# A quantised attention loop: VectorE's copy of turned codes behind a step's second maximum, and a bias addition moved from that loop to the feed-forward

## The reference, cut to what matters

```python
q = quant_act(q, q_alpha, q_zp, 4) * SCALE
k = quant_act(k, k_alpha, k_zp, 4)
v = quant_act(v, v_alpha, v_zp, 4)
attn = jnp.einsum('bhnd,bhmd->bhnm', q, k)
attn = jax.nn.softmax(attn, axis=-1)
attn = quant_act(attn, attn_alpha, attn_zp, 8)   # clip(round(attn / alpha + zp)) to 8 bits
out = jnp.einsum('bhnm,bhmd->bhnd', attn, v)
out = out.transpose(0, 2, 1, 3).reshape(B, N, C)
y = jnp.einsum('bnc,oc->bno', out, wp) + proj_b
...
x = x + y          # x is the program's input
```

## Time and profile before

| what | value |
|---|---|
| median of 3 runs | 777.06 us (776.28 to 779.78) |
| the profiled execution | 775.85 us, span from first to last instruction 774.1 us |
| busy share of the span | PE 81%, DVE 70%, ACT 65%, POOL 31% |
| stage B | from 199.6 us (first scores) to 338.5 us (end of the last codes) |

### The profile page before, as it was taken

How to read it: one execution, slowest core, us unless ns; L and a number is a source line. 1 busy time by engine, 2 the same in 40 slices (tenths; PEclk the granted TensorE clock), 3 DMA queues, 4 the chain that set the end, 5 groups by cost and what they waited for, 6 DMA issues and landing times.

```text
span 774.1 us, 13306 instructions
## 1 busy us (share of the span) xinstructions
PE 626.8 (81%) x4818; PEld 378.4 (49%) x4818; DVE 544.9 (70%) x1123; ACT 501.2 (65%) x1189; POOL 236.1 (31%) x237
## 2 busy tenths in 40 slices
PE   7579987686688988985898978778688889677986
PEld 3322223264255655662655545454467655355754
DVE  7784326737899988958877777649984556977554
ACT  5459997654577877842567657739468547758752
POOL 5030006003388977983200000000154300035410
PEclk9769997899755555577579999989679899969989
DMA  9400000000000000000000000000000000000000
GB/s 283 158 1 1 1 1 1 0 1 0 1 2 1 1 1 1 1 2 0 1 1 2 1 1 2 2 0 1 0 2 2 2 1 0 1 1 2 3 1 27
DMA packets 9204, 9.88 MB, mean 13 GB/s; under 512 B 2890, under 2 KB 7988, under 8 KB 9012
## 3 DMA queue, kind: packets, MB, share of 16 engines
q1 hardware_dynamic: 9140, 9.04, 3.6%
HBM read 8.51 MB, written 0.52 MB: 12 GB/s over the span
## 4 chain that ended last, share of the span: by engine, by line
PE 44%; DVE 34%; ACT 11%; issue 8%; POOL 1%; DMA 1%; ACTq 0%; DVEq 0%; POOLq 0%
PE ps L1452 5%; PE ps L1712 4%; DVE s_nmB L1095 4%; PE ps L1615 4%; PE ps L1695 3%; ACT arena L578 3%; PE ps L1732 3%; PE ps L1523 2%; PE ps L1806 2%; PE ps L1602 2%; PE ps L1495 2%; PE ps L1917 2%; DVE s_nmD L1366 2%; PE ps L1854 2%; PE ps L1440 2%
## 5 line engine op out<-in xcount | busy, mean ns | idle before, releaser
L422 POOL TENSOR_SCALAR arena<-arena,s_rB,s_zpu 128x512 uint8<-128x512 f32 x128 | 116.0, 944 | 34.7 <-DVE s_rB L1068 33.9
L616 ACT ACTIVATE arena<-ps,s_nmB 128x512 f32<-128x512 f32 x128 | 86.6, 683 | 31.4 <-DVE s_nmB L1095 30.8
L638 ACT ACTIVATE arena<-ps,s_nmx 128x512 f32<-128x512 f32 (+3 forms) x128 | 60.7, 527 | 50.1 <-DVE s_nmx L1193 49.7
L1095 DVE TENSOR_REDUCE s_nmB<-ps 128x2 f32<-128x1024 f32 x64 | 77.3, 1217 | 6.6 <-PE ps L1602 6.2
L456 POOL COPY arena<-arena 64x512 f32<-64x512 f32 x16 | 12.4, 773 | 217.5 <-PE ps L1799 215.6
L1188 DVE TENSOR_REDUCE s_nmx<-ps 128x1 f32<-128x512 f32 (+3 forms) x128 | 56.6, 483 | 21.4 <-PE ps L1698 20.9
L578 ACT ACTIVATE arena<-ps 128x1024 f32<-128x1024 f32 x64 | 60.9, 1026 | 6.9 <-PE ps L1507 6.8
L1458 PE MATMUL ps<-ones 128*128 128x512 f16 x150 | 44.2, 446 | 24.0 <-ACT s_rn L569 3.6
L1615 PE MATMUL ps<-cst,arena 128*128 128x128 f32 x256 | 61.0, 417 | 1.7 <-POOL arena L422 0.8
L1615 PEld LDWEIGHTS ps<-cst,arena 128*128 128x128 f32 x256 | 48.8, 218 | 14.7 <-POOL arena L422 8.2
L1602 PE MATMUL ps<-staged 8*128 8x512 f16 x128 | 45.8, 580 | 12.4 <-ACT arena L616 11.5
(11 more groups left out here) (337 smaller groups left out, 1508.0 us busy)
## 6 DMA issues: line engine op xcount, KB each, us to landing
w_d<-in_wqkv SPq DMA_DIRECT2D x2, 768.0 KB
vec<-in_vec SPq DMA_DIRECT2D x1, 1200.0 KB, 10.5
vec<-in_vec SPq DMA_DIRECT2D x1, 960.0 KB, 8.1
w_h<-in_w SPq DMA_DIRECT2D x2, 341.0 KB
x_tok<-in_x SPq DMA_DIRECT2D x1, 512.0 KB, 3.9
arena<-in_w_f SPq DMA_DIRECT2D x2, 256.0 KB, 7.8
rope<-in_rope SPq DMA_DIRECT2D x1, 512.0 KB, 8.9
w_do<-in_wo SPq DMA_DIRECT2D x2, 256.0 KB
```

The source lines that it names most:

```text
L422: nc.gpsimd.tensor_scalar(u8[:, n % 4, j // 2, :, 2 * (j % 2)], prob[:, n % 2, j * 512:j * 512 + 512], sm("rB", 8)[:, c:c + 1], sm("zpu", ...
L616: nc.scalar.activation(prob[:, n % 2, j * 512:j * 512 + 512], ps[:, j, :], ACT.Exp, bias=sm("nmB", 8)[:, c:c + 1], accum_out=sm("sumB", 8) ...
L638: nc.scalar.activation(probC[:, n % 2, at(qt):at(qt) + w], ps[:, bank, col:col + w], ACT.Exp, bias=nmx[:, TB * b + qt, h:h + 1]).then_inc( ...
L1095: free(V.tensor_reduce(sm("nmB", 8)[:, c:c + 2], ps[:, 2 * half:2 * half + 2, :], X, ALU.max, negate=True), "maxB")
```

## The change

On VectorE, `codes_half(n - 3)` moves out of the loop over the two halves, so that it stands behind the second maximum instead of between the rates and the second maximum. And the two additions x + proj_b leave steps 9 and 10 of stage B and stand in stage M, behind the evacuations of the first feed-forward matrix. No instruction is added or taken away, and the streams of PE, ACT, POOL and SP are the same, instruction by instruction.

```diff
@@ stage M @@
                 taken(t, V.scalar_tensor_tensor(out=hid1[:, t, :], in0=ps[:, t % 6, :], scalar=sm("us")[:, t:t + 1],
                                                 in1=v_("b_f1"), op0=ALU.mult, op1=ALU.add))
+            for b in range(B):
+                xb = x[:, TB * b:TB * b + TB, :]
+                add(xb, xb, per_tile(v_("proj_b"), TB))
             dve.wait_ge(sem["fn"], 1)
@@ stage B, step n @@
                         if half == 0 and n >= 1:
                             rates(n - 1)
-                        if half == 0 and n >= 3:
-                            codes_half(n - 3)
+                    if n >= 3:
+                        codes_half(n - 3)
...
                     if n == H + 6:
                         values_b(0)
-                    if n in (9, 10):
-                        xb = x[:, TB * (n - 9):TB * (n - 8), :]
-                        add(xb, xb, per_tile(v_("proj_b"), TB))
                     if n == 3:
                         scale_b(1)
```

## The result

The changed kernel took 780.16 us in the median of 20 runs (777.28 to 783.42), the kernel before 775.43 in 20 runs on the same chip (773.56 to 779.78). The ratio of the means is 1.0057, with 95% interval [1.0041, 1.0073]: slower by 4.4 us of 775.4 (3.2 to 5.7). The forecast, +3.3 us on 777.06, is a ratio of 1.0043.

The account below looks back on a forecast made before the run. It took TensorE at 1.2 GHz to bound stage B, three other engines nearly as full; +4.0 for the copy and -0.7 for the additions gave +3.3 on 777.06, so 780.4 us, range 774 to 785.5.

Parts of the forecast that it names:

- The maximum loop: Stage B, two-step loop through VectorE, ScalarE and TensorE: with the copy 7.60 us, 8.20 in the group-copy step.
- the count over four steps: Stage B from a group-copy step: four steps take 16.05 instead of 15.47, so the copy's 0.58 is paid once.
- Eight steps times 0.5: Stage B steps 3, 5, 7, 10, 14, 18, 20, 22 pay 0.5 each, +4.0; 6 and 26 nothing.
- The additions: Leaving stage B's steps 9 and 10 gives -0.7 us, bounds 0 and -1.4; in stage M's idle gap they cost nothing.
- Zero for the transposes: Stage B: the moved copy ends before TensorE's second half of transposes needs it, so no cost was taken.
- one of the prediction's own signs of being wrong: In the changed kernel's profile: a wait of TensorE's transposes on VectorE's copy appears.
- The spare of 0.12: Stage B: copy ends at S + 1.89, TensorE needs it at S + 2.01, S being its second scores' end.
- The rival: Stage B: transposes wait for the copy, 0.2 in each of 29 steps, +5.8 more, 786 us; chance 0.13.
- TensorE's waits on exponentials: Stage B: TensorE's stops for ScalarE, 11.5 us before, would grow by about 4.
- The faster rival: Stage B: earlier second maximum brings rates earlier, GpSimd waits less; -3.1, 774.0 us, at most -8.3; chance 0.14.
- GpSimd as the pace: Stage B: GpSimd paces the steps and hides the delay; -0.5, 776.6 us; chance 0.18.
- a floor of 3.79 a step: Stage B: rates cannot overtake codes in flight by the port rule, so GpSimd needs at least 3.79 us a step.

Follow-up runs that it names:

- job steps: Changed kernel, copy behind the second maximum only in steps 3, 5, 6, 7, 10, 14, 18, 20, 22, 26; ratio 1.007, stage B 137.54 us.
- additions only: Changed kernel with the copy of codes back in front of the second maximum; ratio 1.0032 against the kernel before, stage B 133.28 us.
- free steps: Changed kernel, copy behind the second maximum only in the 19 steps without another VectorE job there; ratio 1.0012, stage B 133.70 us.

## Why the prediction was right, point by point

- **The maximum loop** held. Second maximum 0.04 behind its scores (within 0.1 said), next first maximum 0.61 later (0.6), two steps 8.19 (8.20). In the group-copy step, ScalarE's exponentials are what TensorE waits for. What covers the copy in the other steps was named wrongly: not the first maximum's wait, since step 13's first maximum starts 0.72 behind its scores, for 0.18 before. The slack lies behind it, between the exponentials and TensorE's next first scores, as the count over four steps had it (11.10 against 11.70).
- **Eight steps times 0.5** gave the right sum by unequal parts. The delay of the second maximum against before rose by 0.8 at step 3, 0.85 at 5, 0.25 at 7, fell by 0.17 at 10 (0.55 for the copy less the additions' 0.72), rose by 0.69 at 14 and at 18, and by 0 at 20 and 0.1 at 22. That is 3.2, for 3.3 forecast with the additions taken off. One error is in taking a job's own duration as fixed: at steps 3, 5, 7, 20 and 22 it changed with the move (last section). That 6 pays nothing was right, that 26 does was not: it paid 0.54 in "job steps". Its second maximum stood 0.65 behind its scores before only because TensorE ran at 1.00 there; in "additions only", at 0.50, it is 0.10. In the pair of before and after the larger gain of after's own stretch hides this price.
- **The additions** were right: -0.72 for -0.7, and free in stage M.
- **Zero for the transposes** failed in part, and with it one of the prediction's own signs of being wrong came true: TensorE's transposes do wait for VectorE's copy. The spare of 0.12 left out the 0.15 from the copy's end to the fifth transpose, so seven steps waited 0.14 each. Two of these lie in the four steps of the chain above: the first ran ahead of the wait for ScalarE, which took it up (8.19), the second (272.93) is the 0.12 over the forecast's 16.05. The rival had the mechanism; its price, 0.2 in 29 steps or 5.8, is refuted by 7 x 0.14 = 1.0.
- **TensorE's waits on exponentials** grew by 2.2, not by about 4. I had left the additions out of that figure: net, stage B's 3.3 was to be found. Full stops hold 2.2 of it, the seven longer transposes the other 1.0, which the trace counts as busy.
- **The faster rival** fell: GpSimd's waits for rates grew by 5.2. The second maximum came no more than 0.07 earlier in most job steps, since it had stood at its scores already. **GpSimd as the pace** fell too: in steps 3 to 18 each step's price went through, and the next to nothing at steps 20 and 22 is what VectorE's gaps grew by there (0.09 and 0.14), since their jobs got shorter.
- Whole time against sum: +4.4 (3.2 to 5.7) for +3.3. The profiled pair says +3.7, of it 3.28 in stage B. The unchanged part behind stage B differs by up to 5.7 us between these profiles, so a whole time that hit so closely is partly luck. That stage B grew by just 3.3 is partly luck too: at one clock I estimate 3.8 to 4.0 (3.28 + 0.6 by the stretches; 4.26 + 0.42 - 0.72 from "job steps", "free steps" and the additions). The loop and its sign are shown; its price was a sixth or so low.

## What to carry to other kernels

Where several engines are nearly full, ask of a moved instruction which loop between engines it enters, not how long it is: 0.58 us in front of a maximum that waits anyway was free; behind it about 0.55 was paid in those steps in which another job of unchanged length stood in the same gap, and almost nothing in the others. Eleven instructions dealt out one to a step cost less than in lumps of two to four, in part because they got shorter. Look also at what a moved instruction's reader needs: a spare of 0.12 was too little for a handover of 0.15. And when the clock moves whole times by as much as the effect, measure the stage between two of its own instructions.

## What the runs showed of the hardware

VectorE's instructions that read SBUF took other times after the move, by where GpSimd's codes stood. Those with two inputs in SBUF first: the product on 128x80 in step 20, before and after, with the codes that ran then (0.88 each, four in a row):

```profile
286.07 0.75 DVE L764 TENSOR_TENSOR s_colsum<-s_colsum,s_zpa 128x80 f32<-128x80 f32 x1
```

```profile
284.15 3.51 POOL L422 TENSOR_SCALAR arena<-arena,s_rB,s_zpu 128x512 uint8<-128x512 f32 x4 [0.27 <-DVE s_rB L1068]
```

```profile
290.09 0.24 DVE L764 TENSOR_TENSOR s_colsum<-s_colsum,s_zpa 128x80 f32<-128x80 f32 x1
```

```profile
287.61 3.50 POOL L422 TENSOR_SCALAR arena<-arena,s_rB,s_zpu 128x512 uint8<-128x512 f32 x4 [0.27 <-DVE s_rB L1071]
```

Before it ended at 286.82, as the third of the codes did (284.15 + 3 x 0.88 = 286.78); after, at 290.33, the third ended at 290.24 (287.61 + 3 x 0.875 = 290.23). So it took 0.75 or 0.24 as it came early or late in a code. The Trainium skill, "SBUF — State Buffer", section "Who interferes with whom", says that such an instruction and one of GpSimd that reads SBUF exclude each other; the trace agrees, and shows the grain: one code, not four. So the rates, too, are held up by one code and not by the four (their product took 0.36 in the earlier trace rows), and a floor of 3.79 a step does not follow from the port. The first product of the preparation went from 1.03 to 1.35, a product in step 22 from 0.62 to 0.26. Two instructions with one input changed as well: the clip in step 5 from 0.55 to 0.86 and the cast in step 7 from 0.90 to 0.37. In both kernels they end at the same distance behind an instruction of GpSimd (0.4 and 0.15), so the exclusion seems not to be for two inputs alone. These differences are as large as the 0.58 that I was pricing.
